# Attention: reads only in turned form, their variance from squares summed by TensorE, rows centred in the update, logits of two images in one product

## The reference

```python
    def _ln(x):
        m = jnp.mean(x, axis=-1, keepdims=True)
        v = jnp.mean((x - m) ** 2, axis=-1, keepdims=True)
        return (x - m) * jax.lax.rsqrt(v + LN_EPS)
...
    def step(carry, v_prev):
        x_state, rho = carry
        x_update = jax.nn.relu(v_prev @ Dx.T)
        x_t = X_DECAY * x_state + x_update
        x_t = x_t / jnp.maximum(jnp.sum(jnp.abs(x_t), axis=-1, keepdims=True), L1_EPS)
        a_star = jnp.einsum('bdn,bn->bd', rho, x_t)
        y_core = _ln(a_star) @ Dy.T
        y_t = jax.nn.relu(y_core) * jax.nn.relu(x_t)
        v_star = _ln(y_t @ E.T)
        rho_t = U_DECAY * rho + _ln(v_prev)[:, :, None] * x_t[:, None, :]
        return ((x_t, rho_t), v_star)
...
    h = _L0_tok_ref(x, ...)
    h = jnp.concatenate([h, txt], axis=1)
    h = h + _L0_attn_ref(_layernorm(h, axis=-1), L0_attn_E, L0_attn_Dx, L0_attn_Dy)
    h = h + _L0_ffn_ref(_layernorm(h, axis=-1), ...)
```

## Time and profile before

| | us |
|---|---|
| median of 3 runs | 2758.26 (2756.05 to 2761.63) |
| the profiled execution | 2755.14 |
| its span | 2753.4 |
| PE busy | 2334.1 (85%) |
| DVE busy | 1924.8 (70%) |
| ACT busy | 1050.1 (38%) |
| POOL busy | 500.5 (18%) |
| attention stage, from the first memset of DVE to the first of the stage behind it | 1976.1 to 2226.2 |

### The profile page before, as it was taken

How to read it: one execution, slowest core, us unless ns; L and a number is a source line. 1 busy time by engine, 2 the same in 40 slices (tenths; PEclk the granted TensorE clock), 3 DMA queues, 4 the chain that set the end, 5 groups by cost and what they waited for, 6 DMA issues and landing times. The chain is left out here.

```text
span 2753.4 us, 191399 instructions
## 1 busy us (share of the span) xinstructions
PE 2334.1 (85%) x88271; PEld 1444.0 (52%) x88271; DVE 1924.8 (70%) x3293; ACT 1050.1 (38%) x1799; POOL 500.5 (18%) x619
## 2 busy tenths in 40 slices
PE   5799999977999997789999975876499826899998
PEld 3466666644666665456666642222277712444444
DVE  5688888865888886668888854004588863677776
ACT  3433333352333332523333333002136623677776
POOL 1034422200444221024442200000223200000000
PEclk9899999997999999989999997898789958999999
DMA  3266666615999996179999964896234203788886
GB/s 86 57 152 168 170 163 163 170 40 186 322 322 320 313 314 185 58 253 325 328 315 310 311 215 159 314 415 118 81 93 113 66 14 82 125 141 143 144 141 100
DMA packets 243410, 515.84 MB, mean 187 GB/s; under 512 B 65423, under 2 KB 114895, under 8 KB 222223
## 3 DMA queue, kind: packets, MB, share of 16 engines
q1 hardware_dynamic: 233736, 504.07, 64.4%
q10 hardware_dynamic: 9495, 9.34, 1.6%
HBM read 295.39 MB, written 214.78 MB: 185 GB/s over the span
## 5 line engine op out<-in xcount | busy, mean ns | idle before, releaser
L923 ACT ACTIVATE p_v<-p_ps,k_scale_bias 128x1024 f32<-128x1024 f32 x384 | 441.8, 1200 | 883.8 <-PE p_ps L794 883.8
L904 POOL COPY k_xm<-p_sp 64x288 f32<-64x288 f32 x372 | 260.2, 700 | 1181.0 <-DVE p_sp L327 1164.8
L317 DVE STREAM_TRANSPOSE p_vt<-p_v 128x1024 f32<-128x1024 f32 x384 | 451.2, 1213 | 6.4 <-ACT p_v L923 6.4
L794 PEld LDWEIGHTS p_ps<-k_idfty,p_t 32*64 32x64 f32 x24576 | 292.0, 135 | 178.5 <-issue 178.4
L2201 DVE TENSOR_TENSOR x_ht<-x_ht,x_mask 128x384 f32<-128x384 f32 x512 | 262.0, 554 | 149.7 <-ACT x_ht L2172 102.2
L2172 ACT ACTIVATE x_ht<-x_ph,w_b 128x384 f32<-128x384 f32 x576 | 303.4, 578 | 142.4 <-PE x_ph L2224 142.4
L322 DVE STREAM_TRANSPOSE p_at<-p_ps 128x1024 f32<-128x1024 f32 x192 | 228.5, 1228 | 149.6 <-PE p_ps L295 149.6
L794 PE MATMUL p_ps<-k_idfty,p_t 32*64 32x64 f32 x24576 | 319.8, 237 | 10.7 <-issue 10.7
L803 PEld LDWEIGHTS p_ps<-p_vt 128*32 128x32 f32 x24576 | 219.6, 109 | 99.8 <-issue 99.8
L2224 PE MATMUL x_ph<-x_et,w_w 64*64 64x384 f32 x2304 | 247.0, 494 | 12.7 <-DMA x_et<-expert_inputs 6.4
L2240 PE MATMUL x_pe<-x_ht,w_w 64*64 64x384 f32 x2304 | 245.0, 489 | 11.3 <-DVE x_ht L2201 10.2
(11 more groups left out here) (329 smaller groups left out, 2625.4 us busy)
## 6 DMA issues: line engine op xcount, KB each, us to landing
field<-p_v SPq DMA_DIRECT2D x768, 256.0 KB, 5.8
p_v<-field SPq DMA_DIRECT2D x128, 1024.0 KB
x_mask<-expert_weights SPq DMA_DIRECT2D x32, 1536.0 KB, 14.8
l_v<-field SPq DMA_DIRECT2D x16, 2048.0 KB, 25.8
k_xm<-field SPq DMA_DIRECT2D x12, 2048.0 KB, 28.7
at_cf<-state_coefficients SPq DMA_DIRECT2D x32, 384.0 KB
k_mixw<-field SPq DMA_DIRECT2D x4, 2048.0 KB, 26.1
k_mixw<-in_L_tok_fw_dram SPq DMA_DIRECT2D x48, 144.0 KB, 4.4
```

The costliest lines, as they stand in the source:

```text
L317: return nc.vector.transpose(cols(vt), cols(px.rearrange("p (g m) -> p g m", g=G)))
L794: ins = nc.tensor.matmul(ps[64 * a1:64 * a1 + 64, g, col:col + S], lines, K["idfty"][rows, :], start=False, stop=True, skip_group_check=True)
L904: nc.gpsimd.tensor_copy(view[64 * k:64 * k + 64, :, j, :, G * i:G * i + G], sp[64 * j:64 * j + 64, :, :, 16 * k:16 * k + M1].rearrange("p ...
L923: nc.scalar.activation(field[:, 2 * q:2 * q + 2, CH * half:CH * half + CH], ps[:, e, 2 * q:2 * q + 2, :], ACT.Relu, bias=bias, scale=scale ...
```

## The change

The reads are made in turned form only. ACT squares the turned reads out of PSUM (`lq`), and PE multiplies the squares with a small matrix `pairs` that holds 1/64 (`variances`, two images at a time), which gives the variances if the reads are centred. So that they are, `update_phase` subtracts each row's mean on POOL ahead of the product with `rho`. DVE turns the 8 variances into the small constants of the values' norm with one operation; it has no statistics of the reads any more, and the chain of the norms works on 16 columns for two norms. The router's weights are laid out in two column blocks over 128 rows with zeros elsewhere, so that one product gives the logits of two images; ACT copies them in one operation. `variances` stands between the values and the logits in PE's order. Semaphores follow.

```diff
+            act.wait_ge(s.wr_zero, 1)
             for half in range(2):
-                act.dma_start(W["Wr"][D * half:D * half + D, :], d["Wr"]).then_inc(s.const_in, 16)
+                act.dma_start(W["Wr"][D * half:D * half + D, 8 * half:8 * half + 8], d["Wr"]).then_inc(s.const_in, 16)
...
+            ve.memset(W["Wr"][:, :], 0.0).then_inc(s.wr_zero, 1)
...
                 pool.wait_ge(rows_in[g], 32)
-                pool.wait_ge(s.rho_ready, g + 1)
+                pool.wait_ge(s.aggr, 2 * g + 1)
                 if g >= 2:
                     pool.wait_ge(le_out[g % 2], 16)
-                nc.gpsimd.tensor_tensor(le[:, g % 2], h[:, part], spread_over(rho[:, part], D), ALU.mult).then_inc(s.le_ready, 1)
+                nc.gpsimd.tensor_tensor(le[:, g % 2], h[:, part], spread_over(w[:, 0, part], D), ALU.subtract).then_inc(s.le_centred, 1)
+                pool.wait_ge(s.le_centred, g + 1)
+                pool.wait_ge(s.rho_ready, g + 1)
+                nc.gpsimd.tensor_tensor(le[:, g % 2], le[:, g % 2], spread_over(rho[:, part], D), ALU.mult).then_inc(s.le_ready, 1)
...
-    READ, VALUE, ROW = (slice(NB * j, NB * j + NB) for j in range(3))
-    NORM = 10
+    VALUE, ROW = (slice(NB * j, NB * j + NB) for j in range(2))
+    NORM = 9
...
-        st = sb("st", [T, 3 * NB, 6])
-        w = sb("w", [T, 2, 6, 3 * NB])
-        eps = sb("eps", [T, 3 * NB])
+        lq = sb("lq", [P, HT])
+        pairs = sb("pairs", [P, 2])
+        st = sb("st", [T, 2 * NB, 6])
+        w = sb("w", [T, 2, 6, 2 * NB])
+        eps = sb("eps", [T, 2, 2 * NB])
...
-        logits = [t[0:T, HT:HT + 4 * 8] for t in (ps_t, ps_l)]
...
-                    at_least(eng, s.fx_done, k - 1)
+                    at_least(eng, s.t2_done, k - 1)
                     eng.dma_start(le[:, par], le_dram[:, bass.ds(NB * k, NB), :]).then_inc(le_in[par], 16)
...
                     act.wait_ge(s.t2_done, k + 2)
                     nc.scalar.copy(lat[:, 1 - par, :], ps_l[:, 0:HT]).then_inc(s.a2_ready, 1)
+                    act.wait_ge(s.var_done, k + 1)
+                    nc.scalar.activation(lq[:, :], ps_l[:, 0:HT], ACT.Square).then_inc(s.square_ready, 1)
...
                     act.wait_ge(s.um_done, j + 1)
-                    for h in range(2):
-                        nc.scalar.copy(W["gate"][:, bass.ds(NB * j + 4 * h, 4), :], logits[h].rearrange("p (b e) -> p b e", b=4))\
-                            .then_inc(s.sp_ready, 1)
+                    nc.scalar.copy(W["gate"][:, bass.ds(NB * j, NB), :].rearrange("t (h i) e -> t i h e", h=2),
+                                   logits.rearrange("p (i h e) -> p i h e", i=4, h=2)).then_inc(s.sp_ready, 1)
...
             nc.scalar.copy(lat[:, 0, :], ps_l[:, 0:HT]).then_inc(s.a2_ready, 1)
+            nc.scalar.activation(lq[:, :], ps_l[:, 0:HT], ACT.Square).then_inc(s.square_ready, 1)
...
-                at_least(dve, s.fx_done, j)
+                at_least(dve, s.t2_done, j)
...
                 if valid(k):
-                    dve.wait_ge(s.fx_done, k + 1)
-                    stats(ps_a[:, :].rearrange("t (b d) -> t b d", b=NB), READ, s.vt_ready)
+                    dve.wait_ge(s.var_done, k + 1)
+                    ve.tensor_scalar(eps[:, par, VALUE], ps_a[:, 0:NB], EPS, EPS * EPS, ALU.mult, ALU.add).then_inc(s.eps_ready, 1)
...
-                if valid(k):
-                    dve.wait_ge(s.vt_ready, NB * (k + 1))
+                at_least(dve, s.eps_ready, min(k, n) if isinstance(k, int) else k)
                 at_least(dve, s.st_done, min(NB * (2 * k - 1), 2 * NB * n) if isinstance(k, int) else NB * (2 * k - 1))
                 c = Chain(dve, s.step, NORM * k)
-                norm_statistics(nc, c, st, w[:, par], eps[:, :])
+                norm_statistics(nc, c, st, w[:, par], eps[:, 1 - par])
                 dve.sem_inc(s.aggr, 1)
-                c.then(ve.tensor_scalar(eps[:, VALUE], w[:, par, 3, READ], EPS, None, ALU.mult))
...
+            ve.memset(eps[:, :, :], EPS).then_inc(s.w_fix, 1)
+            for h in range(2):
+                for g in range(2):
+                    ve.memset(pairs[D * h:D * h + D, g:g + 1], 1.0 / D if g == h else 0.0).then_inc(s.w_fix, 1)
+            dve.wait_ge(s.w_fix, 7)
...
             def reads(j, par, r, between):
                 pe.wait_ge(le_in[par], 16 * r + 16)
                 at_least(pe, s.a2_ready, j)
-                at_least(pe, s.sp_ready, 2 * (j - 4))
-                at_least(pe, s.vt_ready, NB * j)
+                at_least(pe, s.square_ready, j)
                 for q in range(2):
                     pe.wait_ge(s.s_ready, 2 * j + q + 1)
                     pe.nop(nofuse=True)
@@ -1925,11 +1939,16 @@
                                                start=True, stop=True)
                     if q == 1:
                         ins.then_inc(s.t2_done, 1)
-                    for b in range(4 * q, 4 * q + 4):
-                        ins = nc.tensor.matmul(ps_a[:, D * b:D * b + D], sc[:, T * b:T * b + T], le[:, par, b, :], start=True, stop=True)
-                    if q == 0:
+                    else:
                         between()
-                ins.then_inc(s.fx_done, 1)
+
+            def variances(j):
+                pe.wait_ge(s.square_ready, j + 1)
+                at_least(pe, s.eps_ready, j)
+                pe.nop(nofuse=True)
+                for i in range(4):
+                    ins = nc.tensor.matmul(ps_a[:, 2 * i:2 * i + 2], lq[:, T * i:T * i + T], pairs[:, :], start=True, stop=True)
+                ins.then_inc(s.var_done, 1)
...
                     ins.then_inc(s.ix_done, 1)
+                if valid(k + 1):
+                    variances(k + 1)
                 if valid(j):
                     pe.wait_ge(s.t_ready, j + 1)
-                    if valid(k + 1):
-                        pe.wait_ge(s.a2_ready, k + 2)
                     pe.nop(nofuse=True)
                     for i in range(4):
-                        for h in range(2):
-                            rows = slice(D * h, D * h + D)
-                            ins = nc.tensor.matmul(logits[h][:, 8 * i:8 * i + 8], e2t[rows, 1 - par, T * i:T * i + T], W["Wr"][rows, :],
-                                                   start=True, stop=True)
+                        ins = nc.tensor.matmul(logits[:, 16 * i:16 * i + 16], e2t[:, 1 - par, T * i:T * i + T], W["Wr"][:, :],
+                                               start=True, stop=True)
                     ins.then_inc(s.um_done, 1)
             scores(0, 0)
             reads(0, 0, 0, lambda: None)
+            pe.wait_ge(s.w_fix, 7)
+            variances(0)
...
-    W = {"gate": sb("gate", [T, B, 8]), "Wr": sb("Wr", [P, 8]), "eye": sb("eye", [P, P]), "h2": sb("h2", [T, B, D])}
+    W = {"gate": sb("gate", [T, B, 8]), "Wr": sb("Wr", [P, 16]), "eye": sb("eye", [P, P]), "h2": sb("h2", [T, B, D])}
```

More of the change, by code:

```diff
@@ L261, in __init__ @@
         self.head_scaled = sem("head_scaled")
+        self.square_ready = sem("square_ready")
+        self.var_done = sem("var_done")
+        self.eps_ready = sem("eps_ready")
+        self.wr_zero = sem("wr_zero")
         self.rho_ready = sem("rho_ready")
         self.le_ready = sem("le_ready")
+        self.le_centred = sem("le_centred")
         self.le_out0 = sem("le_out0")
@@ L1556, in variances @@
                 dve.sem_inc(s.aggr, 1)
-                c.then(ve.tensor_scalar(wg[:, 0], wg[:, 3], EPS, None, ALU.subtract))
+                c.then(ve.tensor_scalar(wg[:, 1], wg[:, 3], EPS, None, ALU.subtract))
             def scales(g):
@@ L1563, in scales @@
                 dve.wait_ge(s.scale_ready, g + 1)
-                c.then(ve.tensor_tensor(wg[:, 1], wg[:, 5], wg[:, 5], ALU.mult))
-                c.then(ve.tensor_tensor(wg[:, 1], wg[:, 1], wg[:, 0], ALU.mult))
-                c.then(ve.tensor_scalar(wg[:, 2], wg[:, 1], EPS, None, ALU.add))
+                c.then(ve.tensor_tensor(wg[:, 2], wg[:, 5], wg[:, 5], ALU.mult))
+                c.then(ve.tensor_tensor(wg[:, 2], wg[:, 2], wg[:, 1], ALU.mult))
+                c.then(ve.tensor_scalar(wg[:, 2], wg[:, 2], EPS, None, ALU.add))
                 dve.sem_inc(s.aggr, 1)
@@ L1708, in attention_phase @@
         ps_v = ctx.enter_context(nc.psum_tensor("at_pv", [T, CH], F32))
-        logits = [t[0:T, HT:HT + 4 * 8] for t in (ps_t, ps_l)]
+        logits = ps_t[0:T, HT:HT + NB * 8]
         cf_in, h_in, le_in, e_out = [s.u_in0, s.u_in1], [s.y_in0, s.y_in1], [s.sp_out0, s.sp_out1], [s.u_out0, s.u_out1]
@@ L1885, in _ @@
             ve.memset(w[:, :, :, :], 1.0).then_inc(s.w_fix, 1)
-            ve.memset(eps[:, :], EPS).then_inc(s.w_fix, 1)
-            dve.wait_ge(s.w_fix, 3)
+            ve.memset(eps[:, :, :], EPS).then_inc(s.w_fix, 1)
[3 more added lines that the diff above has]
+            dve.wait_ge(s.w_fix, 7)
             for j in range(2):
@@ L1962, in body @@
                     at_least(pe, s.t_ready, j)
-                    at_least(pe, s.sp_ready, 2 * j)
```

(1 more changed line is left out.)

## The result

The changed kernel takes 2785.38 us in the median (2774.46 to 2791.74, six runs) where the kernel before took 2758.11 in the same series: a ratio of 1.0089, 95% interval 1.0066 to 1.0113. It is slower by 27 us; 2795 was forecast. The profiled execution of the change is the longest of its six, 2791.74, with a span of 2790.0, and 36.6 above that of before.

A forecast was written before the change was run, and what follows sets the result against it. DVE was taken to set the 12.62 us attention tick, with PE nearly full. Chain -1.6, clock +37.6 and attention start +0.5 gave +36.5 on the profiled 2755.1: 2791.6, as a median 2795 us, range 2765 to 2826.

The forecast's parts named there:

- Read statistics, gain 0: DVE in attention: 17.9 us of statistics go, but lie inside the 1.46 us gap up to POOL's result; gain 0.
- Chain of the norms: DVE in attention: 24 to 16 columns saves 0.1 us a tick, -1.6 us in all; ends 0 and -4.3.
- The clock: TensorE in attention: longer idle before the values brings the clock to half repeatedly; +37.6 us, ends 11 and 66.
- the new wait of 1.4 to 1.5 lies between the two that were followed by a fall: PE before the value products: the wait lies between earlier ones of 1.93 and 0.98 us, so falls are expected.
- Count and price: Attention ticks 3 to 14: 8 falls of 12 (ends 4 to 12), at 4.7 us each (ends 2.8 and 5.5).
- the 1.2 taken: Variance and logit products behind the values: at half clock they cost 1.2 us more a fall, from 0 to 2 x 0.7.
- the step from profile to median (+3.1): Whole kernel: median of the runs lies 3.1 us above the profiled execution's 2755.1, taking 2791.6 to about 2795.
- Update stage: Four POOL subtractions of 3.61 us each, covered by DVE's 8.32 us wait for the sums: 0, end +1.
- the clock did not hold: Rival (a), attention: 1.4 us of idle leaves the clock up; 2754 by profile, 2757 for a median; chance 0.18.
- nor were the falls few: Rival (b), attention: one to three falls, 2760 to 2771 us; chance 0.15.
- POOL's addition stayed behind the scan: Rival (c), attention: POOL's sum ready before DVE's scan ends, each tick loses 0.95 us, 2740 to 2743; chance 0.05.
- Joining the logits saved nothing: Rival (d), PE in attention: joining two images' logits saves nothing, 0.70 us against 0.72; in the sum, no chance given.

The follow-up runs named there:

- the two opposite runs: Changed kernel with both groups of row-form read products back, unread: 2751.04 us; kernel before without those products from block 1 on: 2794.00 us.
- one group of products put back: Changed kernel with one of two groups of 8 row-form read products a tick made again, unread: first group 2757.15 us, second 2755.71 us.
- both orders: Changed kernel with variance products ahead of value products on PE, and value statistics ahead of row statistics on DVE: 2775.49 us.
- the variances early: Changed kernel with a block's variance products put ahead of the value products in PE's order, same work: 2772.28 us.
- the run with the centring alone: Kernel before with only POOL's subtraction of the rows' means added in the update stage: 2755.01 us, ratio 0.9992.
- the order alone: Kernel before with only DVE's statistics of the values put ahead of those of the rows: 2751.02 us, ratio 0.9979.
- both groups back: Changed kernel with both groups of row-form read products (2 x 8 a tick) made again on PE, unread: 2751.04 us, ratio 0.9982.
- the two together, with the variances early and one group: Changed kernel with variances ahead of values, value statistics ahead of row statistics, and the second group of row-form read products back: 2744.95 us, ratio 0.9955.
- the run with both orders and the second group: Changed kernel with variances ahead of values, value statistics ahead of row statistics, and the second group of row-form read products back: 2744.95 us.
- the first group put back: Fall at 2126.2: changed kernel, variances ahead of values, value statistics ahead of row statistics, first group of row-form read products back: 2748.74 us.

## Why the prediction was right, and what was mis-sized

*Read statistics, gain 0:* right. Their place is now a wait for POOL of 1.06 to 1.07 us.

*Chain of the norms:* 12.53 to 12.32 is 0.21 a tick (the tick of 12.62 in the earlier trace rows was the longest at full clock), where 0.1 was taken; 16 ticks make 3.4 in place of 1.6, inside the ends.

*The clock:* the mechanism was right, as the two opposite runs show; its reason was only half right. The step "the new wait of 1.4 to 1.5 lies between the two that were followed by a fall" took the length of one wait as the cause. Waits of 1.05 to 1.13 were followed by no fall with one group of products put back; a fall came after nothing longer than 0.79 with both orders (at 2091.1), and after nothing longer than 0.40 with the variances early (at 2070.5); and in the change itself a wait of 1.34 stands ahead of ticks with a fall and without. It forecast well because the removed products lengthen that wait too; that part is luck.

*Count and price:* 9 falls against 8. The twelve ticks took 183.71 where twelve of 12.32 are 147.8: 35.9 over, and part of the ninth fall lies behind them. Where a fall comes in every tick, a tick takes 16.6 to 16.7 (by the starts of the scans 16.8 to 16.9), 4.3 to 4.5 over, against 4.7. Within the price, the values gave less than taken (3.49 to 4.02, one 4.74, against 5.35 and 4.57 of the earlier trace rows), the scores more (3.62 to 5.15). Variances and logits gave 0.60 + 0.61, the 1.2 taken.

*What the sum had left out:* the first tick, 17.37 us (1996.80 to 2014.17) against 12.68, +4.7, and 2.3 more at the end of the stage. The account of the profile is 0.6 for the start, 4.7 and 0.1 for the first two ticks, 31.6 for the twelve (183.71 against 152.16) and 2.3: 39.2, the stage's whole difference. Ahead of the stage 0.8 came in, most of it at the end of the update stage; behind it 3.4 went, in stages that the change does not touch. So 36.6 against a sum of 36.5 is partly luck of terms that cancel.

*Against the median:* 27 us, not 36.5, because the step from profile to median (+3.1) held for before only. The six runs of the change spread over 17 us; the two shortest, 2774.5 and 2775.5, have mean clocks of 0.921 and 0.922, the other four 0.912 to 0.916. Only the profiled run's falls can be counted, and it was the longest.

*Update stage:* the wait for the sums covered most: it shrank from 8.32 to 2.80. It did not cover all: POOL's last product holds the operation behind that wait, 0.90 in place of 0.26. These 0.64 are inside the end of +1, and the median of the run with the centring alone does not show them.

*Rivals:* the clock did not hold, nor were the falls few; POOL's addition stayed behind the scan. Joining the logits saved nothing: 0.76 (2107.37 to 2108.13) against 0.70.

## What to carry to other kernels

Work that lies off the critical path is not free to remove from TensorE: where another engine sets the pace, less work can bring the clock down, as it did here, and the products that are on the path then pay. Ahead of such a change, look for the ticks at half clock that the kernel already has, and test the removal alone, or put dummy products in its place. When the clock is kept up, the order of the waiting engine's steps is worth as much as the work removed from it: the order alone gave a ratio of 0.9979, the work removed with both groups back 0.9982, and the two together, with the variances early and one group, 0.9955.

## What had not been expected of the hardware

DVE's small operations were held by POOL in a place where the kernel before had less of it. In the first tick the scaling of the states falls on the chain of the norms:

```profile
2001.03 3.61 POOL L1763 TENSOR_TENSOR w_x<-w_x,at_cf 128x768 f32<-128x768 f32 x2 [3.73 <-DMA at_cf<-state_coefficients]
2001.24 1.68 DVE L1367 TENSOR_TENSOR at_w<-at_st 96x16 f32<-96x16 f32 x1
2002.96 1.72 DVE L1368 TENSOR_TENSOR at_w<-at_st 96x16 f32<-96x16 f32 x1
...
2014.17 0.16 DVE L1866 TENSOR_SCALAR at_eps<-at_pa 96x8 f32<-96x8 f32 x1 [3.17 <-PE at_pa L1950]
```

Two operations of 0.18 us took 1.68 and 1.72, 3.0 us more, each until one of POOL's two products had ended. Before, one took 1.27 there, so against before this is 1.7 of that tick's 4.7 us. The last row is the other 3.0: DVE waits for the variances, behind values at half clock. At the end of the update stage it was the same:

```profile
1959.44 3.61 POOL L1662 TENSOR_TENSOR up_le<-w_h,up_w 96x2048 f32<-96x2048 f32 x1
1959.56 3.54 DVE L1571 TENSOR_TENSOR up_w<-up_w 96x32 f32<-96x32 f32 x1
...
1967.20 0.90 DVE L1615 TENSOR_TENSOR up_us<-up_us,up_rt 128x96 f32<-128x96 f32 x1 [2.80 <-DMA up_us<-update_sums]
```

The Trainium skill (SBUF — State Buffer, section "Who interferes with whom") says that a DVE operation with two inputs in SBUF contends with a GpSimd operation that reads SBUF, for ports that one of them locks. These rows agree: each of the long DVE operations ends with a product of POOL. Two inputs are not needed for it, though: in the run with both orders and the second group L1369, which has one tensor as input, took 1.67 us in that place in the first tick, in place of 0.17.

What stays open is why ticks of the change with the same wait of 1.34 us differ, some with a fall and some without, and why the clock fell once at 2126.2 with the first group put back. And whether other products, ones that do something useful, could hold the clock up as the dummy ones do was not tried.
